# The cross attention of the second block with keys in rows: a score pass for the maximum, and a second one minus the maximum

## The chip, the core and the metric

The kernel runs as one program on one NeuronCore of a Trainium2 chip. The metric is the device time of the program in microseconds, the median of three runs; lower is better. TensorE multiplies matrices into PSUM, VectorE and ScalarE work elementwise and read PSUM, GpSimd works elementwise in SBUF only, and SyncE issues transfers.

## The reference

Four blocks over x of 64 sequences x 128 tokens x 128 features. Each block adds a cross attention over a context of 120 keys (16 heads of 8 features) and then a mixture of experts; the fourth block also has a self attention. What the change touches is the cross attention of the second block, which has no mask:

```python
# L1: x is normalised first (layernorm without scale), the context is not
q = layernorm(x) @ wq.T + bq          # (64, 128, 128), then 16 heads of 8
k = ctx @ wk.T + bk                   # (64, 120, 128)
v = ctx @ wv.T + bv
s = einsum('bhqd,bhkd->bhqk', q, k) / sqrt(8)      # 64 x 16 x 128 x 120
x = x + (softmax(s) @ v) @ wo.T + bo
```

## The kernel before, in words

The kernel is a list of stages with a barrier between them: load, a0, f0, a1, f1, a2, f2, a3, renorm, s3, f3. The a and s stages are attentions (`attention_phase`), the f stages experts. a1, the second block's cross attention, is the stage in question. x stays in SBUF throughout.

A stage takes its 64 sequences in 16 groups of GB = 4. A sequence has U = 4 units of four heads, so a group has S = 16 steps, and a step s works on sequence s//4, unit s%4. Each engine runs a program of its own, written out by hand slot by slot (`groups_loop`, `group`, `behind`, `work_at`), and they meet in semaphores. Tokens are in rows of the score tile: one score matmul per step gives 128 tokens x (4 heads x 120 keys) in PSUM.

Heads are told apart by masks. The projected queries and keys are split into a high and a low fp32r part (`high_part` on ScalarE, `low_part` on GpSimd), and three terms (high.high, low.high, high.low) are stacked in 3x32 = 96 rows by SyncE (`stack_terms`, 24 small copies per group inside SBUF). GpSimd multiplies the stacked keys by a 0/1 pattern (`masked_keys`, L348), which gives the tile KM, 96 rows x 4 sequences x 480 columns per unit, double buffered.

A step then goes round four engines:

1. TensorE: the score matmul, weights 96x128 (queries), 480 moving columns (masked keys), L786.
2. VectorE: maximum over the keys of each head, L547, and subtraction of it into SBUF, L552 (`softmax_shift`).
3. ScalarE: the exponential, in place in SBUF, L704 (`exponentials`).
4. TensorE, TURN = 2 steps later: four transposes, keys into rows, L801 (`turn`).
5. ScalarE: copy of the transposed tile out of PSUM, L710 (`turned`).
6. TensorE, VALUES = 4 steps later: 4 products with the values and 4 with ones for the denominators, in four column strips of the array, L825 (`values`). Plain f32 products show as two instructions each, so a step has 16.

Per sequence follow a reciprocal (L560), a normalisation (L566) and the output matmul (L839); per group the bias row (L837), the projections of the next group (L751 transposes of the normalised x, L754 q, L758 k, L763 v), the addition to x (L575) and the statistics for the next norm (L580). The score tile SC and the transposed tile TP have two buffers each, PR and PT four, which is what a step may run ahead.

```python
    at_least(pe, sub_ready, n - 1)                 # scores(n): SC[n % 2] is free again
    ...
    pe.wait_ge(exp_ready, n + 1)                   # turn(n)
    ...
    pe.wait_ge(pt_ready, n + 1)                    # values(n)
```

## Time and profile before

| what | value |
|---|---|
| time, median of 3 runs | 4263.11 us (4260.68 to 4274.32) |
| the profiled execution, its own time | 4260.05 us |
| its span, first to last instruction | 4258.2 us |
| TensorE busy | 3539.6 us, 83% |
| VectorE busy | 3346.6 us, 79% |
| ScalarE busy | 2332.4 us, 55% |
| GpSimd busy | 1570.1 us, 37% |
| granted TensorE clock, mean | 0.897 of full |
| stage a1 | 549.5 to 1031.5 us of the span |

In the profile PE is TensorE (MATMUL) and PEld its weight loads (LDWEIGHTS), DVE is VectorE, ACT ScalarE, POOL GpSimd, SPq the transfers that SyncE issues. "out<-in" names the tiles; buffer numbers and the stage's number are left out, so a_ stands for a0, a1, a2 and a3 alike, and a stretch of time tells which stage it is. fp32r matmuls are shown as f32. Matmuls are pipelined: the duration of one is longer than the distance to the next, so distances between starts tell the pace. The median of the runs lies 3 us above the profiled execution.

### The profile page before, as it was taken

Reading aid. Unit: us, or ns where it says so; the run is one execution under the profiler, and the core shown is the slowest. Engines: PE = TensorE matmul, PEld = TensorE weight load, DVE = VectorE, ACT = ScalarE, POOL = GpSimd, SP = SyncE. Lnnn points to the kernel's source line nnn. Section 1 sums busy time; section 2 is a strip of 40 time slices with the busy share of each in tenths; the row PEclk is TensorE's granted clock in tenths of the full one; section 3 lists DMA queues with packets and bytes.
Section 4 is the critical chain, followed back from the end, with each engine's and each line's share of the span. In section 5 each row is a group of like instructions: output and inputs, shape, how many; then the busy total and the mean of one; then the engine's idle time right before and its main releaser. Section 6 shows DMA issues by size and latency. Waiting matters only on the chain. (4 is left out here: it accounts for less than half of the span.)

```text
span 4258.2 us, 95393 instructions
## 1 busy us (share of the span) xinstructions
PE 3539.6 (83%) x31830; PEld 2463.6 (58%) x31831; DVE 3346.6 (79%) x6141; ACT 2332.4 (55%) x4244; POOL 1570.1 (37%) x911
## 2 busy tenths in 40 slices
PE   6983979999599899993058849999499998799999
PEld 3552646667476566662046626666365666677777
DVE  7888879998898788885035578888687877788888
ACT  2432657775376566651035536777566665466665
POOL 2210045553000454533744435554254443222222
PEclk9985989998699899995579969999699999799999
DMA  1002122222000222220112142221221112100000
GB/s 63 16 31 103 76 61 64 62 65 63 13 0 6 63 60 57 60 69 13 52 56 62 57 123 62 58 60 49 69 50 47 46 47 73 40 13 12 15 15 15
DMA packets 158984, 209.04 MB, mean 49 GB/s; under 512 B 37820, under 2 KB 109824, under 8 KB 155585
## 3 DMA queue, kind: packets, MB, share of 16 engines
q1 hardware_dynamic: 150593, 189.40, 16.4%
q0 software_dynamic: 8192, 16.92, 1.2%
q8 instruction: 132, 2.16, 0.2%
q14 instruction: 67, 0.55, 0.0%
HBM read 53.09 MB, written 42.21 MB: 22 GB/s over the span
## 5 line engine op out<-in xcount | busy, mean ns | idle before, releaser
L704 ACT ACTIVATE a_p<-a_p 128x480 f32<-128x480 f32 x832 | 501.8, 603 | 517.7 <-DVE a_p L552 515.2
L348 POOL TENSOR_TENSOR a_km<-a_k,a_slots 96x1920 fp32r<-96x1920 f32 x186 | 631.9, 3416 | 176.9 <-DMA a_k<-a_kh 176.9
L547 DVE TENSOR_REDUCE a_mx<-a_sc 128x4 f32<-128x480 f32 (+1 forms) x832 | 542.6, 652 | 124.4 <-PE a_sc L792 95.1
L552 DVE TENSOR_TENSOR a_p<-a_sc,a_mx 128x480 f32<-128x480 f32 x832 | 531.4, 639 | 18.8
L710 ACT ACTIVATE a_pt<-a_tp 120x512 f32<-120x512 f32 x832 | 487.7, 586 | 81.6 <-PE a_tp L801 76.6
L801 PE MATMUL a_tp<-ident,a_p 128*120 128x128 f32 x3328 | 509.7, 276 | 4.1 <-ACT a_p L704 2.3
L801 PEld LDWEIGHTS a_tp<-ident,a_p 128*120 128x120 f32 x3328 | 399.6, 138 | 90.0 <-ACT a_p L704 27.5
L786 PE MATMUL a_sc<-a_km,a_qr 96*128 96x480 f32 x768 | 395.1, 514 | 32.3 <-DMA a_qr<-a_ql 29.4
L825 PE MATMUL a_nd<-a_pt,a_vm 120*32 120x128 f32 x6656 | 354.6, 285 | 0.0
L825 PE MATMUL a_nd<-a_pt,a_dm 120*32 120x128 f32 x6656 | 334.4, 273 | 0.0
L1767 ACT ACTIVATE f_s<-f_pu 128x512 f32<-128x512 f32 x256 | 153.4, 599 | 212.6 <-PE f_pv L1249 212.6
L547 DVE TENSOR_REDUCE s_mx<-s_sc 128x4 f32<-128x512 f32 x256 | 176.4, 689 | 98.1 <-PE s_sc L792 97.5
L560 DVE RECIPROCAL a_rd<-a_nd 128x128 f32<-128x128 f32 x256 | 242.6, 948 | 6.7 <-PE a_nd L825 6.5
L348 POOL TENSOR_TENSOR s_km<-s_k,s_slots 96x2048 fp32r<-96x2048 f32 x62 | 224.0, 3633 | 52.2 <-DMA s_k<-s_kh 52.2
L704 ACT ACTIVATE s_p<-s_p 128x512 f32<-128x512 f32 x256 | 161.2, 630 | 146.3 <-DVE s_p L552 144.8
L1653 POOL TENSOR_TENSOR f_ya<-f_ya,f_yg 128x512 f32<-128x512 f32 x96 | 125.0, 1302 | 302.4 <-DVE f_yg L1703 302.3
L1678 DVE TENSOR_TENSOR f_a<-f_s,f_pv 128x512 f32<-128x512 f32 x256 | 175.3, 685 | 76.2 <-ACT f_s L1767 68.6
L1690 DVE TENSOR_TENSOR f_al<-f_a,f_ah 128x512 fp32r<-128x512 f32 x256 | 229.2, 895 | 0.0
L786 PEld LDWEIGHTS a_sc<-a_km,a_qr 96*128 96x128 f32 x768 | 146.0, 190 | 137.6 <-issue 128.8
L825 PEld LDWEIGHTS a_nd<-a_pt,a_vm 120*32 120x32 f32 x6656 | 131.2, 108 | 141.6 <-issue 132.3
L2078 PE MATMUL f_px<-ident,f_xr 128*128 128x128 f32 x128 | 25.0, 328 | 226.1 <-DMA f_xr<-dispatched 226.1
L825 PEld LDWEIGHTS a_nd<-a_pt,a_dm 120*32 120x32 f32 x6656 | 199.1, 110 | 0.0
(429 smaller groups left out, 8911.6 us busy)
## 6 DMA issues: line engine op xcount, KB each, us to landing
a_qr<-a_qh SPq DMA_DIRECT2D x384, 64.0 KB, 2.0
a_k<-a_kh SPq DMA_DIRECT2D x384, 60.0 KB, 2.0
a_ctx<-in_ctxT SPq DMA_DIRECT2D x64, 240.0 KB, 2.7
a_qr<-a_ql SPq DMA_DIRECT2D x192, 64.0 KB, 2.0
a_k<-a_kl SPq DMA_DIRECT2D x192, 60.0 KB, 2.0
dispatched<-f_empty SPq DMA_DIRECT2D x8, 1040.0 KB, 21.1
f_xr<-dispatched SPq DMA_DIRECT2D x32, 260.0 KB, 2.6
chosen<-f_none SPq DMA_DIRECT2D x8, 1024.0 KB, 11.9
```

The source lines that it names most:

```text
L348: v.tensor_tensor(KM[par][:, i, :, :].rearrange("p b (j k) -> p b j k", k=KN), K3[:, i, :, :].unsqueeze(2).to_broadcast([TR, GB, 4, KN]), ...
L547: v.tensor_reduce(mx[:], view, AX.X, ALU.max).then_inc(mx_ready, 1)
L552: v.tensor_tensor(PR[s % 4][:].rearrange("p (h k) -> p h k", k=k), view, mx[:].unsqueeze(2).to_broadcast([P, heads, k]), ALU.subtract).the ...
L560: v.reciprocal(RD[:], ND[bt % 2][:, 1, :]).then_inc(rd_ready, 1)
L704: a.activation(PR[s % 4][:], PR[s % 4][:], ACT.Exp).then_inc(exp_ready, 1)
L710: a.activation(PT[s % 4][0:KN, :], TP[s % 2][0:KN, :], ACT.Copy).then_inc(pt_ready, 1)
L786: last = t.matmul(SC[s % 2][:, 0:W], queries, keys, start=True, stop=not masked)
L801: last = t.transpose(TP[s % 2][0:KN, q * P:(q + 1) * P], PR[s % 4][:, q * KN:(q + 1) * KN], R.ident[:])
L825: last = t.matmul(ND[j % 2][32 * q:32 * q + 32, what, :], w, PT[s % 4][0:KN, q * P:(q + 1) * P], start=(what == 0 and i == 0), stop=(i == ...
L1678: v.tensor_tensor(A[s % 2][:], S[s % 2][:], PV[s % 2][:], ALU.mult).then_inc(Z["a_ready"], 1)
L1690: v.tensor_tensor(AL[s % 4][:], A[s % 2][:], AH[s % 4][:].bitcast(F32), ALU.subtract).then_inc(Z["lo_ready"], 1)
L1767: a.activation(S[s % 2][:], PU[s % 2][:], ACT.Silu).then_inc(Z["s_ready"], 1)
```

## The change

a1 gets a function of its own, `turned_attention_phase`. All other stages keep `attention_phase`; the remaining lines of the diff outside it are indentation.

In the new stage the stacked queries are masked instead of the keys (`masked_queries`, 96 rows x 4 units x 4 heads x 128 tokens per sequence, tile QM), and the stacked keys (KS) are used as they are. Each step has two score passes. In the first (`scores`), four matmuls, one per head, with masked queries as weights and 120 keys moving, give the same score tile as before, of which VectorE takes only the maximum. The 16 maxima of a sequence are transposed on TensorE (`maxima_turn`), negated by VectorE (`negated`) and copied by a transfer that ScalarE issues (`negated_in`) into row 96 of QM; row 96 of KS holds ones. In the second pass (`weigh`, 9 steps later), one matmul with the keys as weights and 512 query columns moving gives scores minus the maximum with the keys in rows. ScalarE takes the exponential straight from PSUM into PT. The subtraction, the four transposes and the copy out of PSUM are gone. The stacks go over DRAM (`part_out`, `stack_up`): 4 writes and 6 reads per group in place of 24 copies.

The slots are new too: the products come 11 steps after the scores instead of 4, the output 14 instead of 7; the projections sit in slots 2, 4, 6 and 10 in the order ht, q, k, v; the addition to x in slot 14 and all four statistics in slot 15.

```diff
+def turned_attention_phase(nc, R, I, name, wq, wk, wv, wo, bq=None, bk=None, bv=None, bo=None, own_keys=False, mask=None,
+                           causal=None, ln=None):
...
+    TR = 3 * 32
+    KR = TR + 1
+    U = 4
+    S = GB * U
+    LN_SLOTS = (0, 0, 0, 1)
+    SUM_SLOT, STATS_SLOTS = 14, (15, 15, 15, 15)
+    TURN, NEGATE, WEIGH, VALUES, RECIP, OUTPUT = 5, 6, 9, 11, 12, 14
+    KN = P if own_keys else KC
+    W = 4 * KN
+    steps_of = ["ht", "q", "k", "v"]
+    slot_of = dict(zip(steps_of, (2, 4, 6, 10)))
+    masked = mask is not None or causal is not None
...
+        KS = [sb(n_(f"ks{i}"), [KR, U, GB, KN], F32R) for i in range(2)]
+        QS = sb(n_("qs"), [TR, U, GB, P])
+        QM = [sb(n_(f"qm{i}"), [KR, GB, U, 4, P], F32R) for i in range(2)]
...
+        MX = [sb(n_(f"mx{i}"), [P, 16]) for i in range(2)]
+        NEG = [sb(n_(f"neg{i}"), [16, P], F32R) for i in range(2)]
...
+        SC = [ps(n_(f"sc{i}"), [P, 512]) for i in range(2)]
+        ST = [ps(n_(f"st{i}"), [P, 512]) for i in range(2)]
...
+                def part_out(step, g, par, which, part):
+                    buffer = R.parts[step][par, which, :, 0:part.shape[1]]
+                    sp.dma_start(buffer, part[:].bitcast(F32)).then_inc(parts_out[step], 16)
+                def stack_up(step, g, par, out, cols_of, order):
+                    sp.wait_ge(parts_out[step], 32 * (g + 1))
+                    for term, which in enumerate(order):
+                        src = R.parts[step][par, which, :, 0:cols_of].rearrange("(i r) c -> r i c", r=32)
+                        sp.dma_start(out[32 * term:32 * term + 32], src).then_inc(stack_in[step], 16)
+                def stack_terms(g, par):
+                    sp.wait_ge(high_ready["q"], g + 1)
+                    part_out("q", g, par, 0, HIGH["q"])
+                    sp.wait_ge(low_ready["q"], g + 1)
+                    part_out("q", g, par, 1, LOW["q"])
+                    sp.wait_ge(high_ready["k"], g + 1)
+                    part_out("k", g, par, 0, HIGH["k"])
+                    sp.wait_ge(low_ready["k"], g + 1)
+                    part_out("k", g, par, 1, LOW["k"])
+                    at_least(sp, qm_ready, g * GB)
+                    stack_up("q", g, par, QS[:].rearrange("p i b t -> p i (b t)"), GT, (0, 0, 1))
+                    at_least(sp, st_ready, (g - 1) * S)
+                    stack_up("k", g, par, KS[par][:].bitcast(F32).rearrange("p i b k -> p i (b k)"), W, (0, 1, 0))
...
+                def masked_queries(g, par, b):
+                    at_least(pool, st_ready, (g - 2) * S + (b + 1) * U)
+                    nc.gpsimd.tensor_tensor(QM[par][0:TR, b, :, :, :],
+                                            QS[:, :, b, :].unsqueeze(2).to_broadcast([TR, U, 4, P]),
+                                            slots[:].unsqueeze(1).unsqueeze(3).to_broadcast([TR, U, 4, P]),
+                                            ALU.mult).then_inc(qm_ready, 1)
...
+                def prepare(g, par):
+                    low_part("q", g)
+                    low_part("k", g)
+                    pool.wait_ge(stack_in["q"], 48 * (g + 1))
+                    for b in range(GB):
+                        masked_queries(g, par, b)
+                prepare(0, 0)
+                groups_loop(pool, lambda g, par, first, last: None if last else prepare(g + 1, 1 - par), 3)
...
+                def maxima(g, s):
+                    n = g * S + s
+                    j, i = s // U, s % U
+                    dve.wait_ge(sc_ready, n + 1)
+                    if i == 0:
+                        at_least(dve, mt_ready, g * GB + j - 1)
+                    v.tensor_reduce(MX[j % 2][:, 4 * i:4 * i + 4], SC[s % 2][:, 0:W].rearrange("p (h k) -> p h k", k=KN), AX.X,
+                                    ALU.max).then_inc(mx_ready, 1)
...
+                def negated(b, bt):
+                    dve.wait_ge(mt_ready, b + 1)
+                    if not isinstance(b, int) or b >= 2:
+                        dve.wait_ge(neg_in[bt % 2], (b - bt % 2) * 8)
+                    v.tensor_scalar(NEG[bt % 2][:], ND[(bt + 1) % 2][0:16, 2, :], -1.0, None, ALU.mult).then_inc(neg_ready, 1)
...
+                def negated_in(b, bt, par):
+                    act.wait_ge(neg_ready, b + 1)
+                    act.dma_start(QM[par][TR:KR, bt, :, :, :].rearrange("p i j t -> p (i j t)").bitcast(F32),
+                                  NEG[bt % 2][:].bitcast(F32)).then_inc(neg_in[bt % 2], 16)
+                def exponentials(g, s):
+                    n = g * S + s
+                    act.wait_ge(st_ready, n + 1)
+                    at_least(act, pv_done, n - 3)
+                    a.activation(PT[s % 4][0:KN, :], ST[s % 2][0:KN, :], ACT.Exp).then_inc(exp_ready, 1)
...
+                def scores(g, s, par):
+                    n = g * S + s
+                    j, i = s // U, s % U
+                    if i == 0:
+                        pe.wait_ge(qm_ready, g * GB + j + 1)
+                    if s == 0:
+                        pe.wait_ge(stack_in["k"], 48 * (g + 1))
+                    at_least(pe, mx_ready, n - 1)
+                    if masked:
+                        t.matmul(SC[s % 2][:, 0:W], R.ident_bf[:], addm[:].unsqueeze(1).to_broadcast([P, 4, KN]), start=True,
+                                 stop=False, skip_group_check=True)
+                    for h in range(4):
+                        last = t.matmul(SC[s % 2][:, h * KN:(h + 1) * KN], QM[par][0:TR, j, i, h, :], KS[par][0:TR, i, j, :],
+                                        start=not masked, stop=True, skip_group_check=True)
+                    last.then_inc(sc_ready, 1)
+                def weigh(g, s, par):
+                    n = g * S + s
+                    j, i = (s // U) % GB, s % U
+                    if i == 0:
+                        b = g * GB + s // U
+                        pe.wait_ge(neg_in[j % 2], (b + 2 - j % 2) * 8)
+                    at_least(pe, exp_ready, n - 1)
+                    last = t.matmul(ST[s % 2][0:KN, :], KS[par][:, i, j, :],
+                                    QM[par][:, j, i, :, :].rearrange("p h t -> p (h t)"), start=True, stop=not masked)
+                    if masked:
+                        last = t.matmul(ST[s % 2][0:KN, :], R.ident_bf[0:KN, 0:KN],
+                                        addm_t[0:KN, :].unsqueeze(1).to_broadcast([KN, 4, P]), start=False, stop=True)
+                    last.then_inc(st_ready, 1)
...
+                def values(g, s, par, last):
+                    n = g * S + s
+                    j, i = (s // U) % GB, s % U
+                    if s % S == 0:
+                        pe.wait_ge(ready["v"], g + s // S + 1)
+                    pe.wait_ge(exp_ready, n + 1)
+                    if i == 0:
+                        at_least(pe, ct_ready, g * GB + s // U - 1)
+                        if not (last and s // U == GB - 1):
+                            pe.wait_ge(neg_ready, g * GB + s // U + 2)
+                    for what in range(2):
+                        for q in range(4):
+                            h = 4 * q + i
+                            w = DM[0:KN, i, :] if what else VM[par][0:KN, j, 32 * h:32 * h + 32]
+                            last = t.matmul(ND[j % 2][32 * q:32 * q + 32, what, :], w,
+                                            PT[s % 4][0:KN, q * P:(q + 1) * P],
+                                            start=(what == 0 and i == 0), stop=(i == U - 1), skip_group_check=True,
+                                            tile_position=(0, 32 * q))
+                    last.then_inc(pv_done, 1)
...
+                def maxima_turn(b, bt):
+                    pe.wait_ge(mx_ready, b * U + U)
+                    at_least(pe, ct_ready, b - 2)
+                    t.transpose(ND[(bt + 1) % 2][0:16, 2, :], MX[bt % 2][:], R.ident[:]).then_inc(mt_ready, 1)
...
+                def behind(g, s, par, first, last):
+                    if s - WEIGH < S and not (first and s < WEIGH):
+                        weigh(g, s - WEIGH, par if s >= WEIGH else 1 - par)
+                    if s - VALUES < S and not (first and s < VALUES):
+                        values(g, s - VALUES, par if s >= VALUES else 1 - par, last)
+                    u = s - TURN
+                    if u % U == 0 and u < S and not (first and u < 0):
+                        maxima_turn(g * GB + u // U, (u // U) % GB)
+                    u = s - OUTPUT
+                    if (u + 1) % U == 0 and u < S and not (first and u < 0):
+                        gg = g if u >= 0 else g - 1
+                        output(gg, g * GB + u // U, (u // U) % GB)
...
+        R.parts = {w: nc.dram_tensor(f"parts_{w}", [2, 2, P, GT], F32).ap() for w in "qk"}
...
-        attention_phase(nc, R, I, "a1", I["L1_xattn_wq"], I["L1_xattn_wk"], I["L1_xattn_wv"], I["L1_xattn_wo"],
-                        I["L1_xattn_bq"], I["L1_xattn_bk"], I["L1_xattn_bv"], I["L1_xattn_bo"])
+        turned_attention_phase(nc, R, I, "a1", I["L1_xattn_wq"], I["L1_xattn_wk"], I["L1_xattn_wv"], I["L1_xattn_wo"],
+                               I["L1_xattn_bq"], I["L1_xattn_bk"], I["L1_xattn_bv"], I["L1_xattn_bo"])
```

## Rows read from the trace of the kernel before

**Rows 1.** The page, busy time, share of the span, instructions of each engine.
```profile
PE 3539.6 (83%) x31830; PEld 2463.6 (58%) x31831; DVE 3346.6 (79%) x6141; ACT 2332.4 (55%) x4244; POOL 1570.1 (37%) x911
```

**Rows 2.** Windows of stage a1: ends, length, busy time by engine, PEclk, DMA share, GB/s.
```profile
549.50:578.90 29.40, 7.13 (x16) 3.48 (x16) 13.46 (x21) 6.00 (x8) 15.13 (x12) 0.50 0.28 68
578.90:1021.80 442.90, 436.94 (x5664) 298.08 (x5664) 415.27 (x783) 316.03 (x582) 240.68 (x91) 0.99 0.25 61
1021.80:1031.50 9.70, 5.73 (x99) 3.94 (x98) 5.86 (x13) 3.10 (x6) 0.00 (x0) 0.87 0.01 2
700.40:728.33 27.93, 27.59 (x364) 18.84 (x363) 26.30 (x51) 20.06 (x38) 15.92 (x6) 1.00 0.26 63
```

**Rows 3.** Groups of instructions by form, window 600 to 1000 (in a1).
```profile
L348 POOL TENSOR_TENSOR a_km<-a_k,a_slots 96x1920 fp32r<-96x1920 f32 x59 | 198.6, 3388 | 46.0 <-DMA a_k<-a_kh 46.0
...
L552 DVE TENSOR_TENSOR a_p<-a_sc,a_mx 128x480 f32<-128x480 f32 x229 | 145.5, 635 | 3.2
L801 PE MATMUL a_tp<-ident,a_p 128*120 128x128 f32 x916 | 140.9, 276 | 3.9 <-ACT a_p L704 2.2
...
L710 ACT ACTIVATE a_pt<-a_tp 120x512 f32<-120x512 f32 x230 | 133.7, 581 | 0.0
...
L560 DVE RECIPROCAL a_rd<-a_nd 128x128 f32<-128x128 f32 x58 | 54.9, 947 | 0.0
```

**Rows 4.** Timeline of TensorE, a plain step, and the next group's first score.
```profile
700.40 0.46 PE L786 MATMUL a_sc<-a_km,a_qr 96*128 96x480 f32 x1
700.70 0.60 PE L801 MATMUL a_tp<-ident,a_p 128*120 128x128 f32 x4
701.23 0.42 PE L825 MATMUL a_nd<-a_pt,a_vm 120*32 120x128 f32 x8
701.47 0.40 PE L825 MATMUL a_nd<-a_pt,a_dm 120*32 120x128 f32 x8
701.80 0.48 PE L786 MATMUL a_sc<-a_km,a_qr 96*128 96x480 f32 x1
...
728.33 0.46 PE L786 MATMUL a_sc<-a_km,a_qr 96*128 96x480 f32 x1
```

**Rows 5.** Timeline of TensorE, v projection and a step that waits.
```profile
714.82 1.13 PE L763 MATMUL a_pj<-a_wv,a_ctx 128*120 128x128 f32 x8
715.71 0.46 PE L786 MATMUL a_sc<-a_km,a_qr 96*128 96x480 f32 x1
...
717.36 0.47 PE L786 MATMUL a_sc<-a_km,a_qr 96*128 96x480 f32 x1
717.93 0.65 PE L801 MATMUL a_tp<-ident,a_p 128*120 128x128 f32 x4
...
719.23 0.49 PE L786 MATMUL a_sc<-a_km,a_qr 96*128 96x480 f32 x1
```

**Rows 6.** Timeline of TensorE in f0, fp32r matmuls of 512 columns.
```profile
435.80 0.39 PE L1246 MATMUL f_pu<-f_xh,f_uplo 128*128 128x512 f32 x1
436.03 0.40 PE L1249 MATMUL f_pu<-f_xl,f_uphi 128*128 128x512 f32 x1
```

**Rows 7.** Router of f1: timeline, line view (ns min/median/max), window with PEclk.
```profile
1040.50 1.73 PE L1043 MATMUL f1r_lg<-f1r_wr,f1r_hs 128*128 128x16 f32 x8
...
L1043 PE MATMUL f1r_lg<-f1r_wr,f1r_hs x128: 234/374/389, 1037.9 to 1075.5; 128*128 128x16 f32 x128
...
1037.90:1075.50 37.60, 37.60 (x185) 37.60 (x184) 20.73 (x57) 12.32 (x30) 5.26 (x2) 0.50 0.29 113
```

**Rows 8.** DMA issues of the whole span: count, KB each, median us to landing.
```profile
f_kept<-out_x SPq DMA_DIRECT2D x16, 256.0 KB, 2.8
out_x<-f_kept SPq DMA_DIRECT2D x16, 256.0 KB, 2.3
```

**Rows 9.** Tile view of s_km (ns min/median/max).
```profile
L348 POOL TENSOR_TENSOR s_km<-s_k,s_slots x62: 3592/3599/5642, 3050.0 to 3560.4; 96x2048 fp32r<-96x2048 f32 x62
```

More of the change, by code:

```diff
@@ L2142, in build @@
         gated_rows_phase(nc, R, I, "f0", "proto")
-        attention_phase(nc, R, I, "a1", I["L1_xattn_wq"], I["L1_xattn_wk"], I["L1_xattn_wv"], I["L1_xattn_wo"],
-                        I["L1_xattn_bq"], I["L1_xattn_bk"], I["L1_xattn_bv"], I["L1_xattn_bo"])
+        turned_attention_phase(nc, R, I, "a1", I["L1_xattn_wq"], I["L1_xattn_wk"], I["L1_xattn_wv"], I["L1_xattn_wo"],
+                               I["L1_xattn_bq"], I["L1_xattn_bk"], I["L1_xattn_bv"], I["L1_xattn_bo"])
         gated_rows_phase(nc, R, I, "f1", "shared")
         attention_phase(nc, R, I, "a2", I["L2_xattn_W_q"], I["L2_xattn_W_k"], I["L2_xattn_W_v"], I["L2_xattn_W_o"],
-                        I["L2_xattn_b_q"], I["L2_xattn_b_k"], I["L2_xattn_b_v"], I["L2_xattn_b_o"], mask=I["mask"])
+                               I["L2_xattn_b_q"], I["L2_xattn_b_k"], I["L2_xattn_b_v"], I["L2_xattn_b_o"], mask=I["mask"])
         dispatched_experts_phase(nc, R, I, "f2")
         attention_phase(nc, R, I, "a3", I["L3_xattn_Wq"], I["L3_xattn_Wk"], I["L3_xattn_Wv"], I["L3_xattn_Wo"],
-                        causal=I["causal_ctx"])
+                               causal=I["causal_ctx"])
         renorm_phase(nc, R, out)
         attention_phase(nc, R, I, "s3", I["L3_ffn_wq"], I["L3_ffn_wk"], I["L3_ffn_wv"], I["L3_ffn_wo"],
-                        bo=I["L3_ffn_bo"], own_keys=True, causal=I["causal_own"],
-                        ln=(I["L3_ffn_ln1_scale"], I["L3_ffn_ln1_shift"]))
+                               bo=I["L3_ffn_bo"], own_keys=True, causal=I["causal_own"],
+                               ln=(I["L3_ffn_ln1_scale"], I["L3_ffn_ln1_shift"]))
         gated_outputs_phase(nc, R, I, "f3", "swiglu", out)
```

360 lines of the change are left out of this document (added).

## The prediction

> **What bounds the kernel now.** I read the page first. TensorE is busy for 83% of the span and VectorE for 79% [rows 1], an average over eleven stages, of which the change touches one. So the second view was the table of windows for that stage, a1 [rows 2]. It starts at 549.5, its first score matmul starts at 578.9, its last at 1021.8, and it ends at 1031.5. Between the first and the last score TensorE is busy 436.94 of 442.90 us at the full clock (granted 0.99) and VectorE 415.27. One group of four sequences, from the score at 700.40 to the one sixteen steps later at 728.33, takes 27.93 us, with TensorE busy 27.59 and VectorE 26.30. TensorE sets the pace here, and VectorE is so close behind that relieving it alone can give back only the few places where TensorE waits for it.
>
> Third, the timeline of TensorE through one step without extra work [rows 4]. The score matmul starts at 700.40, the four transposes at 700.70, the values products at 701.23, the denominators at 701.47, the next score at 701.80. So a step is 0.30 + 0.53 + 0.57 = 1.40 us. Inside it: 480 fp32r columns at the 0.23 us for 512 of [rows 6] stream in about 0.20, so 0.10 of the 0.30 is a switch. The four transposes show 0.60 us with a mean of 0.276 each [rows 3, 4], so they start (0.60-0.276)/3 = 0.108 apart, 0.43 for the four, and again 0.10 of the 0.53 is the switch to the next form.
>
> The extra work of a group is priced by [rows 5]: the eight instructions of the v projection take 715.71-714.82 = 0.89 us, or 0.111 for a plain f32 instruction of 128 columns. The q projection (2x512 columns) is then 0.89, k 0.83, v 0.89, the four outputs (8 instructions) 0.89, the four H transposes 0.43, the bias row (512 bf16 columns) 0.23: 4.16 us. With 16x1.40 = 22.4 this makes 26.6, and 27.93-26.6 = 1.3 us of a group are waits. One is shown: the score at 717.36 is followed by transposes only at 717.93 (0.57, not 0.30), and the step takes 1.87 us with nothing extra in it.
>
> **The change part by part.** *VectorE* loses the subtraction, 16 x 0.635 us a group, and ScalarE the copy of the transposed tile, 16 x 0.581 [rows 3]. ScalarE still has the exponential, now out of PSUM (120x512, I take the 0.58 of that copy). VectorE gains one 16x128 negation per sequence. It falls from 26.30 busy to about 26.3-10.2+1 = 17 of 28 us. Both gains lie beside TensorE's work. Worth anything are only the 1.3 us of waits. VectorE's queue gets lumpy, though: slot 15 holds a maximum, a reciprocal (0.947) and four statistics, and slot 0 three normalisations, some 5 us in two steps. Two score buffers cover that by about one step. I credit 1.0 of the 1.3 us.
>
> *TensorE, removed per step*: one score matmul (0.20) and four transposes (0.43). *Added per step*: four score matmuls of 120 columns, each with its own 96x128 weights, and one matmul of 512 fp32r columns with 97x120 weights, 0.23 [rows 6]. The switches (0.10 twice) and the values part (0.57) stay. All hangs on the small matmuls. No fp32r matmul under 480 columns is in the trace. From below: streaming 120 columns at the rate of [rows 6] takes 0.055 each. The next floor is the weight load: the router's instructions stream only 16 columns, yet eight of them take 1.73 us with a mean of 0.374, so start 0.19 apart, at a granted clock of 0.50 [rows 7], about 0.10 at the full clock. Loads and streams overlap at full size, since f32 instructions with 120 weight columns and 128 moving ones come every 0.111 [rows 5]. From above: if fp32r takes four passes at this width, as plain f32 does (two instructions of 0.111 for 128 columns), each costs 0.21. I take 0.111, since the row nearest in both sizes is that of [rows 5], 0.44 a step. New step: 0.44 + 0.10 + 0.23 + 0.10 + 0.57 = 1.44 against 1.40. So +0.04 x 16 = +0.64 a group.
>
> *Turn of the maxima*: one transpose per sequence, 4 x 0.11 = +0.44 a group. Projections and outputs are the same, in other slots.
>
> Sum of a group: +0.64+0.44-1.0 = +0.1 us, and x16 that is +1. The large gain on VectorE goes to an engine that was not the last one.
>
> [...]
>
> *GpSimd*: instead of four masked key tiles of 3.39 us [rows 3] four masked query tiles of 96x2048, 3.60 each [rows 9], so 14.4 + 2.5 for the low parts = 17 of 28 us. Hidden; the first is wanted four slots after it can be ready.
>
> *SyncE's transfers*: 24 small copies a group become 4 writes to DRAM and 6 reads of 240 to 256 KB. Such a write lands in 2.3 us, such a read in 2.8 [rows 8]. The chain q in slot 4, k in slot 6, parts out, stacks in (queued behind each other, k's high and low parts ahead of q's stack), first masked query tile, ends near slot 14; it is needed at slot 16. Hidden; if the cover were gone, every us late would cost 16 us.
>
> *The new wait*: ScalarE waits for the negated maxima, then issues a small copy to row 96. Queued behind that wait are exponentials whose products come two steps later. The copy is issued early in slot 6, and TensorE's second pass needs it in slot 9, about 2.7 steps or 4.5 us later. A 256 KB transfer lands in 2.3 to 2.8, so it is hidden.
>
> *Ends of the stage*: the old one needs 29.4 us before its first score [rows 2]. The new one puts q before k, makes the trip over DRAM and one 3.6 us tile: I estimate +2. In the first group a masked tile every 3.6 us feeds four score steps while no products run yet: three tiles are 10.8 us, against about 8 us of TensorE work in it, so +3. The longer drain shifts work and adds perhaps 1. Together +6, and bounds from 0 to +15.
>
> **Total.** 4260.05 (the profiled execution, span 4258.2) + 1 + 6 = 4267. That execution lies 3 us under the median of the runs, 4263.11, so I forecast 4270.
>
> **The rivals.**
> 1. *The swap is even (my forecast)*, 4270, chance 0.50. Each 0.01 us in a step is 2.6 us of kernel; with +-0.08 in a step, its own range is 4250 to 4295.
> 2. *Narrow fp32r matmuls take four passes*: slower. 0.84 in place of 0.44, +0.40 x 256 = +102 us, less a little if it is one instruction (0.20 each): about 4365. For it: every plain f32 row costs that. Against: at 480 and 512 columns fp32r takes one pass. It decides from about 0.16 us per matmul on. Chance 0.25.
> 3. *The weight load isn't hidden behind 50 ns of streaming*: 0.16 each, +0.2 x 256 = +51, 4320. Against: [rows 5]. Chance 0.08.
> 4. *The negated row comes late*: the copy queues behind 768 KB of stack reads. TensorE stops at the second pass once landing takes over some 4.5 us; each us more is up to 64 us of kernel; 4285 to 4330. Chance 0.07.
> 5. *Weight loads don't set the pace*: 0.055 to 0.08 each, -0.12 to -0.22 a step: 4213 to 4240. [...] Chance 0.10.
>
> **How the numbers follow.** Within 0.3% (13 us) is about what a measurement of this kernel can't tell from no change. Of rival 1's 0.50, 0.14 falls below 4250, 0.25 within, 0.11 above. Faster: 0.14+0.10 = 0.24. Same: 0.25. Slower: 0.11+0.25+0.08+0.07 = 0.51. The likeliest single case is no change, though slower ones hold more in sum. The range 4235 to 4370 holds rival 1, 3, 4 and about half of 2 and of 5, some 0.82. Its upper part is there for rival 2.
>
> **What would show it.** In the profile of the changed kernel: the four score matmuls of a step starting 0.11 apart (0.20 for rival 2, 0.16 for 3, under 0.09 for 5); the second pass followed by the products after about 0.33; a plain step of 1.44, a group of 28.0; VectorE near 60% busy with long waits for TensorE, and no second-pass matmul that waits for the copy from the ACT queue (rival 4). The first score should start about 31 us into the stage. The prediction is wrong if TensorE is no longer near full between first and last score, or if the narrow matmuls are not paced by weight loads.

## The result, and the profile after

The changed kernel takes 4417.83 us (median of four runs, 4415.73 to 4433.86) against 4262.05 for the kernel before: ratio 1.0367, 95% interval 1.0336 to 1.0398. It is 156 us slower, above the end of the range (4370). The profiled execution took 4433.86 us with a span of 4432.1.

The page of the changed kernel, and its windows of stage a1: up to the first score, first to last score, the rest, and one group of sixteen steps (columns as in [rows 2]):

```profile
PE 3677.3 (83%) x31895; PEld 2559.9 (58%) x31895; DVE 3275.7 (74%) x5949; ACT 2207.1 (50%) x3988; POOL 1585.0 (36%) x913
...
549.50:580.83 31.33, 7.17 (x16) 3.51 (x17) 8.70 (x18) 3.96 (x7) 9.68 (x11) 0.50 0.48 122
580.83:1218.00 637.17, 574.38 (x5608) 395.30 (x5608) 346.48 (x584) 193.08 (x322) 261.67 (x93) 0.72 0.26 66
1218.00:1239.50 21.50, 17.22 (x220) 10.11 (x216) 8.29 (x20) 6.30 (x11) 0.00 (x0) 0.74 0.01 2
855.57:898.06 42.49, 41.21 (x370) 27.88 (x366) 21.66 (x40) 12.59 (x22) 17.74 (x7) 0.64 0.29 70
```

From first to last score the stage takes 637.17 us against 442.90 [rows 2], 194 more. TensorE's idle time in it grew from 6 to 63 us; the other 137 us of the loss are busy time. The granted clock fell from 0.99 to 0.72. So the loss is first a clock, and only then waits. f1 begins at 1241.0, before it was 1033.1: +208. Later s3 gives 35 back (563.4 us before, 528.4 after), though the change doesn't touch it. Every other stage is equal within 5 us.

Where the clock is full, TensorE's timeline shows the step that the prediction priced. Beside [rows 4]:

```profile
719.68 0.66 PE L1361 MATMUL a_sc<-a_ks,a_qm 96*128 96x120 f32 x4
720.17 0.45 PE L1373 MATMUL a_st<-a_qm,a_ks 97*120 97x512 f32 x1
720.55 0.42 PE L1396 MATMUL a_nd<-a_pt,a_vm 120*32 120x128 f32 x8
720.79 0.40 PE L1396 MATMUL a_nd<-a_pt,a_dm 120*32 120x128 f32 x8
721.12 0.66 PE L1361 MATMUL a_sc<-a_ks,a_qm 96*128 96x120 f32 x4
```

A plain step is 1.44 us. The four narrow matmuls and the switch after them take 0.49, the second pass with its switch 0.38, the values part 0.57. At half clock the same step takes 2.56 to 2.58.

**Wait N, the negated row.** The same trace, transfers and TensorE in slots 10 to 14 of a group, then what the transfer from the ACT queue did over the stage, and the window after the stop:

```profile
721.63 1.35 SPq L1014 DMA_DIRECT2D a_qs<-parts_q  x3
...
723.26 1.25 SPq L1014 DMA_DIRECT2D a_ks<-parts_k  x3
...
723.86 0.55 ACTq L1274 DMA_DIRECT2D a_qm<-a_neg  x1
...
728.01 0.66 PE L1361 MATMUL a_sc<-a_ks,a_qm 96*128 96x120 f32 x4
...
731.18 0.49 PE L1373 MATMUL a_st<-a_qm,a_ks 97*120 97x512 f32 x1 [2.51 <-DMA a_qm<-a_neg]
...
  PE a_st L1373: 23.2, 14
...
DMA to landing us min/median/max: 1.8/1.8/7.8
...
731.18:763.00 31.82, 31.82 (x241) 21.12 (x245) 15.31 (x27) 9.45 (x16) 13.44 (x6) 0.52 0.05 19
```

The copy of 8 KB usually lands in 1.8 us. Once a group, in all but the first two and the last, it is issued within 1 us of the last of six reads of about 250 KB each, and then it takes 5.9 to 7.8. The second pass of slot 13 stands still for 2.5 us. What follows costs more: TensorE is busy 31.82 of the next 31.82 us, without a gap, at a granted clock of 0.52. Not every such stop lowers the clock: those at 979.14, 1017.02, 1054.08, 1091.85 and 1129.03, of 1.17 to 1.75 us, left it full.

**Wait H, the normalised x.** In groups that N did not leave at half clock another engine is late. VectorE, GpSimd and TensorE of the same trace, and the normalisation over the stage (ns min/median/max):

```profile
1051.60 14.27 POOL L1067 TENSOR_TENSOR a_qm<-a_qs,a_slots 96x2048 fp32r<-96x2048 f32 x4 [6.16 <-DMA a_qs<-parts_q]
...
1060.38 5.83 DVE L151 TENSOR_SCALAR a_h<-x,a_mean,a_rstd 128x128 f32 x3
...
1067.18 1.09 PE L1327 MATMUL a_pj<-ident,a_h 128*128 128x128 f32 x4 [4.13 <-DVE a_h L151]
...
L151 DVE TENSOR_SCALAR a_h<-x,a_mean,a_rstd x60: 329/335/3693, 582.5 to 1141.6; 128x128 f32 x48, 128x128 f32<-128x128 f32 x12
...
L1067 POOL TENSOR_TENSOR a_qm<-a_qs,a_slots x64: 3594/3597/3598, 577.0 to 1177.2; 96x2048 fp32r<-96x2048 f32 x64
```

GpSimd masks four tiles back to back for 14.27 us. A normalisation that VectorE starts in that time takes up to 3.69 us in place of 0.34; the longest in the stage before was 0.99. TensorE waits 4.1 us for it. In this trace 24 normalisations of the stage take over 0.5 us, and each of them ends 0.08 to 0.09 us after one of GpSimd's masked tiles ends. The longest, 3.69 us, is about one masked tile (3.60). That GpSimd's tiles hold the normalisations up is my inference from these lengths and ends; the trace doesn't show by what.

### The profile page after: what moved, and what is told of

Same layout as the page of the kernel before. It is cut to its first block and busy times, and to the rows that moved or that the text cites. A ratio compares the mean times of both kernels' runs of the same rounds, so it can differ in the third digit from the quotient of the medians.

```text
span 4432.1 us, 94510 instructions
## 1 busy us (share of the span) xinstructions
PE 3677.3 (83%) x31895; PEld 2559.9 (58%) x31895; DVE 3275.7 (74%) x5949; ACT 2207.1 (50%) x3988; POOL 1585.0 (36%) x913
## 5 line engine op out<-in xcount | busy, mean ns | idle before, releaser
L704 ACT ACTIVATE a_p<-a_p 128x480 f32<-128x480 f32 x576 | 347.2, 603 | 387.0 <-DVE a_p L552 385.6
L348 POOL TENSOR_TENSOR a_km<-a_k,a_slots 96x1920 fp32r<-96x1920 f32 x124 | 421.2, 3417 | 117.2 <-DMA a_k<-a_kh 117.2
L547 DVE TENSOR_REDUCE a_mx<-a_sc 128x4 f32<-128x480 f32 (+1 forms) x576 | 375.8, 652 | 113.0 <-PE a_sc L792 99.1
L552 DVE TENSOR_TENSOR a_p<-a_sc,a_mx 128x480 f32<-128x480 f32 x576 | 368.3, 639 | 14.7
L801 PE MATMUL a_tp<-ident,a_p 128*120 128x128 f32 x2304 | 352.4, 276 | 0.0
L1141 DVE TENSOR_REDUCE a_mx<-a_sc 128x4 f32<-128x480 f32 x256 | 166.8, 652 | 216.4 <-PE a_sc L1361 216.1
L1281 ACT ACTIVATE a_pt<-a_st 120x512 f32<-120x512 f32 x256 | 152.4, 595 | 331.9 <-PE a_st L1373 331.9
L1067 POOL TENSOR_TENSOR a_qm<-a_qs,a_slots 96x2048 fp32r<-96x2048 f32 x64 | 228.3, 3597 | 105.3 <-DMA a_qs<-parts_q 92.6
L1361 PE MATMUL a_sc<-a_ks,a_qm 96*128 96x120 f32 x1024 | 231.9, 363 | 10.0 <-POOL a_qm L1067 9.9
L1361 PEld LDWEIGHTS a_sc<-a_ks,a_qm 96*128 96x128 f32 x1024 | 186.1, 252 | 69.9 <-issue 61.0
```

The lines of the kernel that those rows point to most:

```text
L348: v.tensor_tensor(KM[par][:, i, :, :].rearrange("p b (j k) -> p b j k", k=KN), K3[:, i, :, :].unsqueeze(2).to_broadcast([TR, GB, 4, KN]), ...
L547: v.tensor_reduce(mx[:], view, AX.X, ALU.max).then_inc(mx_ready, 1)
L552: v.tensor_tensor(PR[s % 4][:].rearrange("p (h k) -> p h k", k=k), view, mx[:].unsqueeze(2).to_broadcast([P, heads, k]), ALU.subtract).the ...
L704: a.activation(PR[s % 4][:], PR[s % 4][:], ACT.Exp).then_inc(exp_ready, 1)
L801: last = t.transpose(TP[s % 2][0:KN, q * P:(q + 1) * P], PR[s % 4][:, q * KN:(q + 1) * KN], R.ident[:])
L1067: nc.gpsimd.tensor_tensor(QM[par][0:TR, b, :, :, :], QS[:, :, b, :].unsqueeze(2).to_broadcast([TR, U, 4, P]), slots[:].unsqueeze(1).unsque ...
```

## The experiments

All keep the rest of the kernel as it is. The table has the ratio to the kernel before, the start of f1 (the end of a1; what lies ahead of a1 agrees within 3 us in all of them) and the length of s3. e7 to e9 ran twice each, the others four to seven times. The two right columns are read in one profiled execution of each kernel, and that lies up to 18 us from the kernel's median (16 above it for the change, 18 below for e1, 11 above for e2, 18 above for e3). Part of this is in f2, which no edit touches: from its start to a3's first score the kernels need 606 to 623 us. So a difference of under some 20 us in f1's start says little by itself.

| kernel | median us | ratio, 95% | f1 starts | s3 |
|---|---|---|---|---|
| before | 4262.05 | | 1033.1 | 563.4 |
| the change | 4417.83 | 1.0367 (1.0336 to 1.0398) | 1241.0 | 528.4 |
| e1_no_row | 4385.26 | 1.0296 (1.0264 to 1.0328) | 1177.8 | 528.1 |
| e2_norm_on_act | 4380.52 | 1.0242 (1.0182 to 1.0303) | 1195.2 | 527.6 |
| e3_both | 4226.09 | 0.9904 (0.9887 to 0.9921) | 1043.4 | 527.9 |
| e4_paced | 4254.32 | 0.9970 (0.9958 to 0.9981) | 1058.9 | 527.5 |
| b1_stall | 4325.90 | 1.0137 (1.0120 to 1.0154) | 1097.7 | 563.5 |
| e5_twice | 4434.78 | 1.0406 (1.0350 to 1.0462) | 1228.6 | 530.5 |
| e6_warm | 4298.30 | 1.0091 (1.0057 to 1.0125) | 1058.0 | 572.5 |
| b2_peel | 4230.41 | 0.9910 (0.9892 to 0.9928) | 1035.0 | 527.9 |
| e7_stop13 | 4472.04 | 1.0484 (1.0434 to 1.0534) | 1279.0 | 528.8 |
| e8_stop13_wide | 4297.36 | 1.0075 (1.0045 to 1.0104) | 1109.2 | 530.6 |
| e9_stop3 | 4340.70 | 1.0176 (1.0117 to 1.0235) | 1154.1 | 527.9 |

### Which wait: N, H or both

**e1_no_row.** The second pass uses 96 rows; the maximum is still taken, turned, negated and copied, but not subtracted.

```diff
-                    if i == 0:
-                        pe.wait_ge(neg_in[j % 2], (b + 2 - j % 2) * 8)
-                    last = t.matmul(ST[s % 2][0:KN, :], KS[par][:, i, j, :],
-                                    QM[par][:, j, i, :, :]...
+                    last = t.matmul(ST[s % 2][0:KN, :], KS[par][0:TR, i, j, :],
+                                    QM[par][0:TR, j, i, :, :]...
```

> Edit: the second pass reads 96 rows instead of 97 and does not wait for the negated maxima (left out: the subtraction of the maximum, so the exponentials are those of the raw scores; the copy of the negated maxima is still made). Theory A (two waits per group stop TensorE, the late copy of the negated row in slot 13 and the normalisation of the next x in slot 1 held up by GpSimd; after each the granted clock is at half for part of the group): the wait in slot 13 is gone, the one in slot 1 stays and now meets the full clock in every group, so a group takes about 36 us instead of 39.8 and the kernel 4340 to 4400. Theory B (the mix of narrow matmuls itself lowers the granted clock): the clock between first and last score stays near 0.7 and the time within 40 us of the changed kernel, above 4380. Theory C (each narrow matmul costs more than 0.12 us): plain steps at full clock above 1.5 us.

**e2_norm_on_act.** ScalarE normalises x in slot 0, as scale and bias of one activation per sequence.

```diff
-                                if LN_SLOTS[j] == s:
-                                    ln_sequence(g + 1, j)          # VectorE
+                        if not last and s == 0:
+                            ln_group(g + 1)                        # ScalarE
+                        ins = a.activation(H[:, j, :], R.x[:, b, :], ACT.Identity,
+                                           scale=norm.rstd[:, bass.ds(b, 1)], bias=shift[:, bass.ds(b, 1)])
```

> Edit: the normalisation of the next group's x is done by ScalarE instead of VectorE. Theory A: the wait of TensorE for a_h in slot 1 is gone, but the late negated row in slot 13 stays, and with it the half clock afterwards in every group: a group near 41 us, the kernel 4400 to 4440, no gain worth the name. Theory B: the same time. Only a theory in which the slot 1 wait is the main cost would give under 4360.

**e3_both.** Both edits; the maximum is again not subtracted.

> Edit: both of the edits above together (the subtraction of the maximum is left out). Theory A: no wait longer than 1 us is left, the granted clock is at full from first to last score, a plain step takes 1.44 us, a group about 28.2 us, the kernel 4255 to 4290, so the two waits interact: the sum of the two gains taken alone is far less than the gain together. Theory B: the clock stays near 0.7 with no waits, 4370 or more. Theory C: full clock, but steps over 1.5 us.

Alone, the edits bring f1 63 and 46 us forward; together 198. By the medians of the whole kernels it is 33 and 37 us, and together 192. They aren't additive because one stop a group is enough. In e1 the transposes of the normalised x wait in most groups (the rows of that line, matmuls and weight loads counted together); in e2 the second pass still waits. e2's median is faster than the 4400 to 4440 that I expected: in four of its groups the row was in time or its stop left the clock full. e3 is faster than expected (4255 to 4290), by what s3 gives. The windows are of e2 and e3, from where the first group ends to near the last score, and one group of e3:

```profile
L1327 PE MATMUL a_pj<-ident,a_h x60: 272/418/475, 592.4 to 1114.2; 128*128 128x128 f32 x60
...
  DVE a_h L151: 90.7, 20
```

```profile
L1384 PE MATMUL a_st<-a_qm,a_ks 97*120 97x512 f32 x256 | 147.5, 576 | 16.2 <-DMA a_qm<-a_neg 16.2
...
634.00:1180.00 546.00, 529.59 (x5310) 362.56 (x5298) 254.57 (x497) 197.72 (x351) 232.42 (x83) 0.72 0.28 71
```

```profile
634.00:1030.00 396.00, 395.24 (x5348) 278.26 (x5340) 253.26 (x499) 197.44 (x353) 233.25 (x83) 1.00 0.38 98
...
869.28:896.57 27.29, 27.25 (x369) 19.18 (x367) 17.39 (x35) 13.93 (x26) 16.78 (x7) 1.00 0.41 103
```

About the same 5,300 matmuls take 546 us in e2 and 396 in e3. TensorE's idle time explains 16 of the 150 us (546.00-529.59); the clock, 0.72 against 1.00, explains the rest. A group of e3 is 27.29 us, against 27.93 [rows 2].

**e4_paced** computes everything: normalisation on ScalarE, and SyncE issues the six reads one per slot instead of in a burst.

```diff
-                        src = R.parts[step][par, which, :, 0:cols_of].rearrange("(i r) c -> r i c", r=32)
+                    if g > 0:
+                        sp.wait_ge(sc_ready, (g - 1) * S + slot + 1)
+                    src = R.parts[step][g % 2, which, :, 0:cols_of].rearrange("(i r) c -> r i c", r=32)
...
+                    stack_up("q", g, qs, GT, 0, 0, 7)      # 8, 9 for the others of q; 11, 12, 13 for k
```

> Edit: a whole kernel, nothing left out. Normalisation on ScalarE, and SyncE issues the six reads of the stacks one per slot (q in slots 7 to 9, k in 11 to 13) instead of all six at once. Theory A with the late row put down to the burst of six reads in front of it: the negated row lands within 4.5 us each time, the wait in slot 13 is under 0.3 us, the clock stays full, 4255 to 4290. If the row is late for another reason than the burst (its 16 small packets into one partition): it stays late and the time is above 4380.

The copy now lands in 4.0 us at worst, and the stops of slot 13 are gone; a group takes 27.36 us (scores at 737.80 and 765.16). Left is the first group at half clock, and one stop of another kind:

```profile
675.55 0.66 PE L1379 MATMUL a_sc<-a_ks,a_qm 96*128 96x120 f32 x4 [1.43 <-DMA a_ks<-parts_k]
...
DMA to landing us min/median/max: 1.8/1.8/4.0
```

After those 1.43 us the steps are slow from 677 to 712. Without the burst, the version that computes everything is a little faster than the kernel before (by 0.3%), but its a1 is 26 us longer; the 35 us of s3, which have another cause (below), make up for it.

### Why a stop of 2 to 4 us costs 10 more

**b1_stall** is the kernel before with one stop a group in a1: in slot 13 TensorE waits for a small copy that ScalarE issues when that slot's score is done.

```diff
+                        if stalled and s == 13:                        # ScalarE
+                            act.wait_ge(sc_ready, g * S + s + 1)
+                            act.dma_start(stall[:], slots[:]).then_inc(stall_in, 16)
...
+                        if stalled and s == 13:                        # TensorE, behind scores()
+                            pe.wait_ge(stall_in, 16 * (g + 1))
```

> Edit: the kernel before, with one wait more per group of a1: in slot 13 TensorE waits behind its score matmul for a small copy that ScalarE issues only when that matmul is done, some 2.5 to 3 us. Theory D (a stop of TensorE costs the new stage so much because its step, with four narrow matmuls paced by weight loads, does not bring the granted clock back, and the old step does within about 5 us): each stop costs itself and 2 to 3 us, 16 of them +60 to +100 us, 4320 to 4365. Theory A as first stated (any such stop costs some nine steps at half clock, whatever the step): +200 us, above 4440.

**e7_stop13** puts the same lines into e3_both.

> Starts from the variant without the negated row and with the normalisation on ScalarE, in which TensorE has no long wait and f1 begins at 1043.4. Adds one stop per group by hand: TensorE waits in slot 13 for a small copy that ScalarE issues once the score of slot 13 is done, the same stop that cost the kernel before about 4 us each (f1 at 1097.7, 2.8 us of it the wait, one or two slower steps after it). The second pass still leaves out the subtraction. Theory D (after a stop the clock stays at half for most of the next group, because the new mix of steps does not bring it back): the stop costs 2.8 us plus some nine steps at 2.5 in place of 1.44, so 10 to 13 us a group, and f1 begins between 1190 and 1240. Rival (what holds the clock down in the changed kernel is something else that goes with the late row, such as the stack transfers or VectorE's queue): 4 us a group as in the kernel before, f1 at 1100 to 1115.

The timeline of TensorE at a stop, and a window after it, in b1_stall and then in e7_stop13:

```profile
892.16 0.65 PE L807 MATMUL a_tp<-ident,a_p 128*120 128x128 f32 x4 [2.64 <-DMA a_stall<-a_slots]
...
894.20:919.80 25.60, 25.32 (x335) 16.97 (x333) 24.55 (x47) 18.74 (x35) 10.73 (x6) 1.00 0.21 51
```

```profile
786.19 0.78 PE L1385 MATMUL a_st<-a_qm,a_ks 96*120 96x512 f32 x1 [2.79 <-DMA a_stall<-a_slots]
...
788.38 1.09 PE L1376 MATMUL a_sc<-a_ks,a_qm 96*128 96x120 f32 x4
...
788.40:812.00 23.60, 23.60 (x180) 15.89 (x179) 9.26 (x19) 8.06 (x15) 7.63 (x4) 0.50 0.00 1
```

Both kernels wait 2.8 us per stop (idle time of TensorE's matmuls and weight loads together, 89.7 and 87.9 us over 32); in b1 it is 2.4 to 2.9 each time, in e7 1.8 to 3.8, because there the copy again follows the burst of reads (landing 1.7/2.7/3.8 us min/median/max, against 1.7/1.8/2.2). The old stage pays 64.6/16 = 4.0 us a stop: 2.8 of wait, and 1.2 that I put down to the clock. The new one pays 235.6/16 = 14.7: 2.8 of wait and 12 of clock; f1, at 1279.0, comes later than theory D had it (1190 to 1240). In the old mix four stops, the one shown among them, leave the clock full, and after the others it is back after one or two steps. In the new one TensorE is busy 23.60 of 23.60 us and stays at 0.50, in eleven of fifteen cases for seven to ten steps, in the others for 13 to 16. This alone makes a stage as slow as the changed kernel's, without the late row and without VectorE's delay.

**e8_stop13_wide** is e7 with one matmul of 480 columns in place of the four narrow ones (one head's queries for all four heads).

```diff
-                    for h in range(4):
-                        last = t.matmul(SC[...][:, h * KN:(h + 1) * KN], QM[par][0:TR, j, i, h, :], KS[par][0:TR, i, j, :], ...)
+                    last = t.matmul(SC[s % 2][:, 0:W], QM[par][0:TR, j, i, 0, :],
+                                    KS[par][0:TR, i, j, :].unsqueeze(1).to_broadcast([TR, 4, KN]), ...)
```

> The same stop in slot 13, and the four 120-column score matmuls of a step are one matmul of 480 columns (the queries of one head as weights, the keys repeated four times: the scores of three heads in four are left out, as is the subtraction). A plain step is then about 1.30 us. Theory D with the narrow matmuls as the cause: steps after the stop are back at the full clock within one or two, as in the kernel before, and the stage is 256 x 0.14 = 36 us shorter for the steps and 64 longer for the stops: f1 at 1065 to 1080. Rival (another part of the new mix holds the clock, or the length of time since the last full stretch): steps of 2.2 to 2.5 us after each stop, f1 at 1150 or later.

TensorE's score matmuls after the stop at 690.54, and the window of the following group:

```profile
696.09 0.78 PE L1385 MATMUL a_st<-a_qm,a_ks 96*120 96x512 f32 x1 [5.07 <-DMA a_stall<-a_slots]
...
698.28 0.75 PE L1375 MATMUL a_sc<-a_ks,a_qm 96*128 96x480 f32 x1
...
700.33 0.49 PE L1375 MATMUL a_sc<-a_ks,a_qm 96*128 96x480 f32 x1
...
701.55 0.49 PE L1375 MATMUL a_sc<-a_ks,a_qm 96*128 96x480 f32 x1
...
721.29:756.90 35.61, 29.77 (x322) 16.81 (x318) 17.20 (x35) 13.85 (x26) 16.76 (x6) 0.76 0.32 82
```

After six of the fifteen stops that a full group follows, the clock is back within one or two steps (1.22 us each at full clock); after the others it takes about five, up to the transposes of slot 2. f1 came at 1109, not at 1065 to 1080, and the waits themselves were longer: the second pass of slot 13 starts 4.3 to 6.3 us behind its score (the last group apart), in e7 2.4 to 4.5. The trace shows why. The steps are shorter, so in most groups the copy of slot 13 is issued 2.9 us behind the last read of the burst, in e7 4.5, and lands later:

```profile
  PE a_st L1385: 71.9, 16
...
DMA to landing us min/median/max: 1.7/4.5/5.8
```

An estimate of e8 without stops is e3's 1043.4 less 256 x 0.22 us for the shorter steps (1.22 against 1.44), 987. A stop then costs (1109.2-987)/16 = 7.6 us: 4.5 of wait (71.9/16) and about 3 of clock, against 12 in e7 and 1.2 in b1. So something about the four narrow matmuls is a large part of the cause, not all of it. The edit also leaves one weight load where there were four, and which of the two counts was not separated.

**e5_twice** is the changed kernel with the matmul of the second pass issued twice, 0.23 us more work a step.

```diff
+                    t.matmul(ST[s % 2][0:KN, :], KS[par][:, i, j, :],
+                             QM[par][:, j, i, :, :].rearrange("p h t -> p (h t)"), start=True, stop=True)
                     last = t.matmul(ST[s % 2][0:KN, :], KS[par][:, i, j, :],
```

> Edit: the changed kernel with the second pass matmul of 512 columns issued twice in every step (the same product, written again: work added, nothing left out). At full clock a step grows by 0.21 us, 3.4 us a group. Theory D: the longer streams bring the clock back sooner, the stretches at half clock after a wait shrink from some 22 us to under 10, and the kernel, with more work in it, is not slower than the changed one: 4340 to 4420. Theory A: the stretches stay as long, each step in them 0.43 longer: 4480 to 4520.

```profile
858.74 0.49 PE L1373 MATMUL a_st<-a_qm,a_ks 97*120 97x512 f32 x1 [0.93 <-DMA a_qm<-a_neg]
...
860.22:867.40 7.18, 7.14 (x94) 4.75 (x93) 6.35 (x13) 2.39 (x4) 7.18 (x3) 1.00 0.01 1
```

A step at full clock is 1.66 us, so the stage has 256 x 0.23 = 59 us more work, and yet f1 starts 12 us earlier. The copy is less late against the slower step (here 0.93 us), and from 800 on the clock stays full after it in seven of ten groups. The whole kernel isn't measurably different from the change (4413.38 to 4464.38 us); its median is 17 us slower and lies between the two theories (4340 to 4420, 4480 to 4520). The stretches at half clock are 10 to 34 us, not all under 10. So e5 says less for theory D than e7 does: it mixes a less late copy with the longer streams.

**e9_stop3** has the stop of e7 in slot 3, just ahead of the plain f32 projections of slots 4 and 6.

> The same stop, but in slot 3, just ahead of the plain f32 projections of slots 4, 6 and 10 (narrow matmuls kept, subtraction left out). If the clock comes back where the plain f32 projections run, as in the changed kernel, it is back by slot 5 or 6: each stop costs 2.8 us and two or three steps at half, about 6 us, and f1 begins at 1130 to 1150. Rival (the time since the stop decides, not what runs in it): nine steps at half wherever the stop stands, f1 at 1190 to 1240 as expected with the stop in slot 13.

```profile
  PE a_st L1385: 28.0, 15
...
DMA to landing us min/median/max: 1.7/1.7/2.4
...
1103.50:1131.40 27.90, 27.90 (x235) 18.99 (x228) 10.62 (x20) 6.48 (x11) 0.00 (x0) 0.50 0.01 1
```

A stop costs (1154.1-1043.4)/16 = 6.9 us here against 14.7. Part of that is the stop itself: no burst stands in front of the copy in slot 3, so it is only 1.9 us long (28.0/15), in e7 2.8. That leaves 5.0 us of clock against 12. In three groups the clock doesn't fall at all; in the others, but for the first and the last, it is back after one to eight steps. The length of the stop is a rival that e9 doesn't rule out by itself. But the shortest stops of e7 (1.80 us in the group at 659, 1.79 in that at 1043, 2.46 in that at 1134) were followed by seven or eight steps at half, so what TensorE does next seems to count, too. The last group of the stage, which has no projections, points the same way: in e9 the clock stays at half to its end after the stop (the window above), and in the changed kernel all sixteen steps of that group, which follows the last late row, run at half:

```profile
1177.22:1218.11 40.89, 40.89 (x333) 27.93 (x329) 15.76 (x32) 8.96 (x15) 3.56 (x2) 0.50 0.01 2
```

In the other groups of the changed kernel, and in most of e7, the clock returns in slots 5 to 8, behind the projections of q and k (two plain f32 instructions of 512 and of 480 columns each).

**e6_warm** is e4 with the k reads one slot earlier and f32 matmuls of 512 columns, whose result isn't used, ahead of and between the first group's steps.

```diff
+                def warm_up(n):
+                    for k in range(n):
+                        t.matmul(ST[k % 2][:], R.ident[:], HT[0][:], start=True, stop=True)
...
+                        if first and s < WEIGH:
+                            warm_up(1)
```

> Edit: the whole kernel with normalisation on ScalarE and paced stack reads (k one slot earlier than in e4_paced, slots 10 to 12), and additional f32 matmuls of 512 columns that nobody reads: five while TensorE waits for the first masked query tile and one in each of the first nine steps. Theory D: the first group of the stage ran at half clock to its end (in e4_paced to 630); with long streams the clock is full by about 590, the stage is 15 to 25 us shorter than in e4_paced and the late k stack near 675 is gone: 4220 to 4240. If the clock of the first group does not answer to that, the time is e4_paced's 4254 or more.

The clock of the first group does answer: it is full by about 592 instead of 630, but TensorE then reaches the later tiles earlier. It stops where three later groups begin (step of 3.18 us at 608.48, 3.00 at 644.89, 2.66 at 708.46) and is back at half each time. f1 starts at 1058.0, as in e4 (1058.9): the gain was given back. The kernel is slower than e4 all the same, by s3's 572.5 us, and far from the 4220 to 4240 that I expected.

### What s3 gave back

**b2_peel** is the kernel before, with three groups of a1 written out ahead of its loop in place of one, as in the changed kernel; it computes the same in the same order, and what lies behind moves to other places in the program.

```diff
-                groups_loop(pe, group, 3 if U == 1 else 1)     # the same on the other engines
+                groups_loop(pe, group, 3 if U == 1 or name == "a1" else 1)
```

> Edit: the kernel before, with three instead of one group of a1 written out ahead of its loop on all engines; the same instructions run, only the code ahead of the later stages is longer. In all kernels with the new a1 the untouched stage s3 is 35 us shorter, because six stops of TensorE of up to 3.9 us at its loop, for which the profile shows no wait, are gone. Theory E (those stops depend on where the code of s3's loop lies): they may vanish or move to another stage, and the time differs from 4262 by more than 10 us either way. Theory F (something that the new a1 leaves behind, data or clock, sets them): s3 is unchanged, 4258 to 4268.

Stage s3 in the kernel before, two stops in TensorE's timeline; and in it and then in b2_peel the score line (after the second bar: idle us before it, and releasers) and a window:

```profile
3156.40 0.79 PE L786 MATMUL s_sc<-s_km,s_qr 96*128 96x512 f32 x1 [3.62 <-issue]
...
3224.63 0.79 PE L786 MATMUL s_sc<-s_km,s_qr 96*128 96x512 f32 x1 [3.54 <-issue]
...
L786 PE MATMUL s_sc<-s_km,s_qr 96*128 96x512 f32 x256 | 139.7, 546 | 33.5 <-issue 22.1 <-DMA s_qr<-s_ql 11.4
...
3056.00:3590.00 534.00, 506.88 (x5936) 327.74 (x5940) 430.20 (x771) 343.92 (x599) 258.42 (x92) 0.95 0.20 48
```

```profile
L786 PE MATMUL s_sc<-s_km,s_qr 96*128 96x512 f32 x256 | 136.3, 533 | 11.6 <-DMA s_qr<-s_ql 11.4
...
3065.00:3570.00 505.00, 496.36 (x5997) 321.60 (x5997) 434.84 (x775) 342.50 (x602) 261.68 (x93) 0.99 0.21 49
```

In the kernel before TensorE stops six times, 22.1 us in all, waiting for nothing that the profile shows. The two stops shown are 68 us apart, two groups, which is one turn of the loop. In b2_peel it doesn't. s3 is 35.5 us shorter, a1 as long as before within 2 us, the kernel 0.9% faster. Nothing but the code ahead of s3 differs between the two, so the 35 us that the change seemed to win in s3 can be had without it, by where the code lies; and e6, whose s3 has six such stops again, shows that they can also be lost (572.5). What at that place stops the engine isn't in the profile.

## Why the prediction was wrong

**The step that failed** is the one headed "The new wait", which ends "so it is hidden", together with rival 4's price. The landing time came from single transfers (2.3 to 2.8); the median copy did even better, 1.8, but the one behind the burst of reads took up to 7.8. I had named that queue in rival 4 and gave it 0.07, with three reads in front (768 KB) where there were six. Its stops alone are cheap: 23.2 us in 14 waits, inside what I had priced. Unpriced was what a stop does to the clock. I took it that TensorE would be back as soon as it worked again, as in the stage before. b1 and e7 measure the two mixes of work: 1.2 us of clock per stop in the old one, 12 in the new one.

**GpSimd "Hidden"** was right for its own queue (14.27 us of a 27 us group), but its tiles delay VectorE's normalisations by up to 3.4 us, where I had looked for lumps in VectorE's own work only. "Two score buffers cover that by about one step" did not help, since the late tile is not a score but the input of the transposes (wait H). e1 shows that H alone keeps the stage at 1177.8.

**Rival 1's arithmetic** held, in part by luck. The narrow matmuls start 0.11 apart and the plain step is 1.44, both as predicted, so rivals 2, 3 and 5 are out. The one pass and four passes of rival 2 are a way to say 0.23 us for 512 fp32r columns [rows 6] and 0.222 for 128 plain f32 ones [rows 5]; no run shows passes. No run shows the 0.08 us either that makes rival 5 end at 4240; in the runs it is 0.11. But two terms of the step are off by 0.05 each and cancel: the narrow matmuls with their switch take 0.49 (the sum had 0.54), the second pass with its switch 0.38 (0.33). A group without stops is 27.36 with everything computed (e4), against 28.0. Its terms without any wait add up to 27.64 (16 x 1.44 + 4.16 + 0.44), so all of the 1.3 us of waits went, where I had credited 1.0, and the priced work took 0.3 less. The 0.374 us of [rows 7] is a median and not a mean, which changes nothing. VectorE falls from 26.30 to 17.39 us a group in e3, 18.7 with the four normalisations that e3 takes from it (predicted 17).

The stage without long waits ends 10.3 us later than before (e3), where the sum had 7. That these are close is luck. From the first score to the third group's e3 needs 68.4 us, the kernel before 56.4: 12 more, since the clock is at half until 634. From there to the last score it is 9.2 faster (377.3 against 386.4), and from the last score to f1 7.3 slower (18.6 against 11.3). So the groups came out better than the +1, and the ends of the stage, priced at +6 with 15 as the bound, at +19.5. e3's 4226 holds the 35 us of s3: beside b2_peel, whose s3 is as short, the new stage is an even swap, as the sum said.

**Not foreseen at all** was s3. The 156 us are about +208 in a1, -35 in s3, and 18 us by which the two profiled executions lie further apart than the two medians.

**The fastest versions** that compute everything are b2_peel (4230.41) and e4 (4254.32); e3 (4226.09) leaves out the subtraction. s3 is equally short in both, and the old a1 ends 24 us before e4's, so the turned form wins nothing yet. Of the 24 us, 15.5 are what e4 has over e3, chiefly in the group behind the stop at 675.55; the rest is in e3 too, whose first group runs at half clock up to 634.

## What to carry to other kernels

Price a possible wait of TensorE as the wait plus the time until its clock is back, and take the latter from the mix of matmuls that follows, not from another stage: here it was 1.2 us in one mix and 12 in the other for stops of 2.8 us on average. A small transfer on a critical edge must not be issued just behind a burst on another queue; spreading six reads over six slots took its worst landing from 7.8 to 4.0 us. Before crediting a gain to a change, compare the stages that it doesn't touch.

## What the runs showed of the hardware that I had not expected

- TensorE was busy without a gap and the clock still did not come back: 23.60 of 23.60 us busy at a granted 0.50 in e7, 31.82 of 31.82 at 0.52 in the changed kernel. It came back sooner with one wide matmul and weight load in place of four narrow ones (e8, about 3 us of clock a stop against 12), and with plain f32 projections close behind a somewhat shorter stop (e9, 5.0 against 12). Why is open.
- Waits as short as 1.43 us were followed by a group at half clock (e4 at 675.55), while one of 2.64 us in the old mix was not (b1 at 892.16), nor five of 1.17 to 1.75 us in the changed kernel itself.
- A VectorE normalisation of 0.34 us took up to 3.69 beside GpSimd's tiles, ten times as long, and ended each time 0.08 to 0.09 us after a tile of GpSimd.
- The loop of s3 stopped TensorE for about 3.7 us at a time with no releaser in the kernel before (22.1 us in six stops), and not at all in b2_peel, where only the code ahead of it is longer.
